# First self attention of a four-layer decoder: scores of each 64-token block only, in both partition halves of a bank

## Time and profile before

| | |
|---|---|
| runs (3), median | 5675.01 us (5669.7 to 5678.21) |
| profiled execution | 5677.53 us |
| its span | 5675.8 us |
| mean granted TensorE clock | 0.904 |
| busy over the span | PE 81%, PEld 48%, DVE 71%, ACT 51%, POOL 47% |
| the changed stage | about 6 to 243 us of the span |

### The profile page before, as it was taken

The page is one execution under the profiler, slowest core; times in us unless marked ns, Lnnn a source line. Parts: engine busy times, 40 slices in busy tenths (PEclk is TensorE's granted clock), DMA queues, the critical chain, the costliest instruction groups (busy, mean ns, idle before and its releaser), DMA issues. The chain is left out here.

```text
span 5675.8 us, 84931 instructions
## 1 busy us (share of the span) xinstructions
PE 4620.5 (81%) x29487; PEld 2737.2 (48%) x29488; DVE 4017.7 (71%) x7585; ACT 2867.0 (51%) x4722; POOL 2669.3 (47%) x2453
## 2 busy tenths in 40 slices
PE   8769999999999999777845776766797679976577
PEld 6555666666666666424632222222464344424344
DVE  4348888888888888576366999999663336548445
ACT  3326777777777777463333545454463325533211
POOL 7437676766776677342074666666432201001100
PEclk9789999999999999887867999999998769977788
DMA  1000000000000000000000000000000000011000
GB/s 21 15 24 1 1 1 25 1 21 1 21 1 21 1 1 5 1 1 2 12 0 14 0 0 0 0 0 0 15 1 1 9 8 19 1 48 25 5 16 7
DMA packets 76485, 49.99 MB, mean 9 GB/s; under 512 B 27879, under 2 KB 71159, under 8 KB 75319
## 3 DMA queue, kind: packets, MB, share of 16 engines
q1 hardware_dynamic: 74039, 43.77, 3.0%
q0 software_dynamic: 2048, 1.05, 0.1%
HBM read 40.18 MB, written 1.18 MB: 7 GB/s over the span
## 5 line engine op out<-in xcount | busy, mean ns | idle before, releaser
L4051 POOL TENSOR_TENSOR l_attn_read<-l_attn_state,l_attn_c_rows 128x1024 f32<-128x1024 f32 x256 | 604.5, 2361 | 329.7 <-DVE l_attn_state L3954 328.7
L2945 POOL TENSOR_TENSOR l_ffn_t<-l_ffn_t 128x512 f32<-128x512 f32 x384 | 489.1, 1274 | 515.2 <-DVE l_ffn_t L2812 515.2
L3954 DVE TENSOR_TENSOR_SCAN l_attn_state<-l_attn_decay,psum 128x1024 f32<-128x1024 f32 x256 | 584.9, 2285 | 8.1
L2546 PE MATMUL psum<-l_ffn_wq,l_ffn_xsT 128*128 128x512 f32 x1152 | 566.2, 600 | 12.4 <-DVE l_ffn_t L2812 10.9
L3756 PE MATMUL psum<-l_attn_read,ident 128*128 128x512 f32 x1024 | 493.0, 604 | 5.4 <-DVE l_attn_yz L3962 3.0
L3747 PE MATMUL psum<-l_attn_parts,pick 96*128 96x512 bf16 x512 | 200.6, 394 | 312.8 <-DVE psum L3946 312.8
L2956 POOL TENSOR_TENSOR l_ffn_p<-l_ffn_p,l_ffn_sm 128x512 f32<-128x512 f32 x384 | 399.6, 1041 | 61.0 <-DVE l_ffn_sm L2844 45.1
L2951 POOL TENSOR_TENSOR l_ffn_t<-l_ffn_t,l_ffn_ss 128x512 f32<-128x512 f32 x384 | 401.0, 1044 | 0.7 <-DVE l_ffn_ss L2827 0.7
L3873 ACT COPY l_attn_c_rows<-psum 128x512 f32<-128x512 f32 x256 | 149.9, 586 | 468.2 <-PE psum L3747 466.7
L2808 DVE TENSOR_TENSOR l_ffn_t<-psum,l_ffn_tab 128x512 f32<-128x512 f32 x384 | 263.6, 686 | 106.5 <-ACT l_ffn_sq L2693 104.7
L3946 DVE TENSOR_TENSOR psum<-psum,l_attn_du 128x1024 f32<-128x1024 f32 x256 | 315.6, 1233 | 32.7 <-POOL l_attn_du L4028 4.6
(11 more groups left out here) (895 smaller groups left out, 11551.8 us busy)
## 6 DMA issues: line engine op xcount, KB each, us to landing
l_ffn_wq<-in_L_ffn_Wqkv SPq DMA_DIRECT2D x6, 1536.0 KB, 6.2
l_xattn_toep<-s4d_taps SPq DMA_DIRECT2D x4, 2048.0 KB, 17.7
l_ffn_wo<-in_L_ffn_Wo SPq DMA_DIRECT2D x6, 512.0 KB, 7.6
l_ffn_w<-in_L_ffn_W SPq DMA_DIRECT2D x6, 341.0 KB
l_ffn_w<-in_L_ffn_w SPq DMA_DIRECT2D x3, 512.0 KB, 4.2
x_all<-in_x SPq DMA_DIRECT2D x4, 256.0 KB, 4.4
l_attn_k<-l_attn_dense_k POOLq DMA_DIRECT2D x64, 16.0 KB, 1.9
l_attn_q<-l_attn_dense_q SPq DMA_DIRECT2D x64, 16.0 KB
```

The costliest lines, as they stand in the source:

```text
L2546: nc.tensor.matmul(ring[it % 2], xsT[:, n % 2, m % G, :], wq[:, z, i * 512:(i + 1) * 512], start=True, stop=True).then_inc(itemed, 1)
L2945: nc.gpsimd.tensor_tensor(t1[:, m % G, i, :], t1[:, m % G, i, :], t2[:, x % 3, :], ALU.add).then_inc(added, 1)
L3954: nc.vector.tensor_tensor_scan(state[:, k % 3, :], decay[:, k % 3, :, :, :].rearrange("p h g t -> p (h g t)"), drive, 0.0, ALU.mult, ALU.a ...
L4051: nc.gpsimd.tensor_tensor(read[:, k % 3, :].rearrange("p (h n) -> p h n", h=2), state[:, k % 3, :].rearrange("p (h n) -> p h n", h=2), row ...
```

## The change

For the local case, each 128 x 128 matrix of scores is replaced by its two diagonal 64 x 64 blocks. Block z (tokens 64z to 64z+63) is written to partitions 64z to 64z+63 of the bank, in columns i*64 to i*64+63 for batch i. A bank then has 256 used columns instead of 512, and each matmul of 128 by 128 becomes two of 64 by 64, for both parts. The mask is 128 x 64 (the same triangle in both halves) and the mask matmuls have 256 columns. VectorE's maximum reads 256 columns. ScalarE's exponential becomes two activations, one for each half of the partitions, which write the diagonal blocks of `pT`. GpSimd sets the whole of `pT` to zero once, behind the masks, and ScalarE waits for that before its first exponential; nobody writes the other blocks afterwards. `value` is as before.

```
-            half_mask, half_mask_t = sb("mask", [128, T]), sb("mask_t", [128, T])
-            mask16, mask_t16 = sb("mask16", [128, T], BF16), sb("mask_t16", [128, T], BF16)
+            half_mask, half_mask_t = sb("mask", [128, CS]), sb("mask_t", [128, CS])
+            mask16, mask_t16 = sb("mask16", [128, CS], BF16), sb("mask_t16", [128, CS], BF16)
...
-                            nc.tensor.matmul(K.bank[n % 2], K.ident16[:], rows(mask16[:], G), start=True, stop=False, skip_group_check=True)
+                            nc.tensor.matmul(K.bank[n % 2][:, 0:G * CS], K.ident16[:], rows(mask16[:], G), start=True, stop=False, skip_group_check=True)
...
-                    for i in range(G):
+                    pieces = [(i, z, slice(CS * z, CS * z + CS)) for i in range(G) for z in range(2)] if local else [(i, 0, slice(0, T)) for i in range(G)]
+                    for i, z, half in pieces:
+                        width = CS if local else NK
...
-                            last = nc.tensor.matmul(K.bank[index(*a) % 2][:, i * NK:i * NK + NK], q4[r, g % 2, s, i * T:i * T + T],
-                                                    k4[r, g % 2, s, i * NK:i * NK + NK], start=not local, stop=True, skip_group_check=local)
+                            keys = k4[r, g % 2, s, i * NK:i * NK + NK]
+                            last = nc.tensor.matmul(K.bank[index(*a) % 2][half, i * width:i * width + width], q4[r, g % 2, s, i * T:i * T + T][:, half],
+                                                    keys[:, half] if local else keys, start=not local, stop=True, skip_group_check=local)
...
-                            last = nc.tensor.matmul(K.bank[2 + index(*b) % 2][:NK, i * T:i * T + T], k4[r, g % 2, s, i * NK:i * NK + NK],
-                                                    q9[r, s, i * T:i * T + T], start=not local, stop=True, skip_group_check=local)
+                            last = nc.tensor.matmul(K.bank[2 + index(*b) % 2][rows_, i * wide:i * wide + wide], keys[:, half] if local else keys,
+                                                    q9[r, s, i * T:i * T + T][:, half], start=not local, stop=True, skip_group_check=local)
...
-                    nc.scalar.activation(pT[:NK, n % 8, :], K.bank[2 + n % 2][:NK, :], ACT.Exp, scale=scale).then_inc(exped, 1)
+                    if local:
+                        if n == 0:
+                            act.wait_ge(masks, 2)
+                        for z in range(2):
+                            half = slice(CS * z, CS * z + CS)
+                            ins = nc.scalar.activation(pT[half, n % 8, :].rearrange("p (b q) -> p b q", b=G)[:, :, half],
+                                                       K.bank[2 + n % 2][half, 0:G * CS].rearrange("p (b q) -> p b q", b=G), ACT.Exp, scale=scale)
+                    else:
+                        ins = nc.scalar.activation(pT[:NK, n % 8, :], K.bank[2 + n % 2][:NK, :], ACT.Exp, scale=scale)
+                    ins.then_inc(exped, 1)
...
-                    ps = K.bank[n % 2][:, :KEYS].rearrange("p (b k) -> p b k", b=G)
+                    ps = K.bank[n % 2][:, :G * (CS if local else NK)].rearrange("p (b k) -> p b k", b=G)
...
-                        build(nc.gpsimd.affine_select(out=full[:], in_=full[:], compare_op=ALU.is_ge, fill=NEG, base=0,
-                                                      pattern=[[sign, T]], channel_multiplier=-sign))
-                        if turned:
-                            build(nc.gpsimd.memset(full[0:CS, CS:T], NEG))
-                        else:
-                            build(nc.gpsimd.memset(full[CS:T, 0:CS], NEG))
+                        for z in range(2):
+                            part = full[CS * z:CS * z + CS, :]
+                            build(nc.gpsimd.affine_select(out=part, in_=part, compare_op=ALU.is_ge, fill=NEG, base=0,
+                                                          pattern=[[sign, CS]], channel_multiplier=-sign))
...
                     nc.gpsimd.memset(to_next[0:CS, CS:T], 0.25 / CS).then_inc(masks, 1)
+                    nc.gpsimd.memset(pT[:], 0.0).then_inc(masks, 1)
```

More of the change, by code:

```diff
@@ L883, in scores @@
                         if local:
-                            nc.tensor.matmul(K.bank[2 + n % 2], K.ident16[:], rows(mask_t16[:], G), start=True, stop=False, skip_group_check=True)
-                    for i in range(G):
+                            nc.tensor.matmul(K.bank[2 + n % 2][:, 0:G * CS], K.ident16[:], rows(mask_t16[:], G), start=True, stop=False, skip_group_check=True)
+                    pieces = [(i, z, slice(CS * z, CS * z + CS)) for i in range(G) for z in range(2)] if local else [(i, 0, slice(0, T)) for i in range(G)]
+                    for i, z, half in pieces:
+                        width = CS if local else NK
                         if a is not None:
@@ L888, in scores @@
                             r = slice(ROW * j, ROW * j + ROW)
-                            last = nc.tensor.matmul(K.bank[index(*a) % 2][:, i * NK:i * NK + NK], q4[r, g % 2, s, i * T:i * T + T],
-                                                    k4[r, g % 2, s, i * NK:i * NK + NK], start=not local, stop=True, skip_group_check=local)
-                            if i == G - 1:
+                            keys = k4[r, g % 2, s, i * NK:i * NK + NK]
+                            last = nc.tensor.matmul(K.bank[index(*a) % 2][half, i * width:i * width + width], q4[r, g % 2, s, i * T:i * T + T][:, half],
+                                                    keys[:, half] if local else keys, start=not local, stop=True, skip_group_check=local)
+                            if (i, z) == pieces[-1][:2]:
                                 last.then_inc(a_done, 1)
@@ L895, in scores @@
                             r = slice(ROW * j, ROW * j + ROW)
-                            last = nc.tensor.matmul(K.bank[2 + index(*b) % 2][:NK, i * T:i * T + T], k4[r, g % 2, s, i * NK:i * NK + NK],
-                                                    q9[r, s, i * T:i * T + T], start=not local, stop=True, skip_group_check=local)
-                            if i == G - 1:
+                            keys = k4[r, g % 2, s, i * NK:i * NK + NK]
+                            rows_ = half if local else slice(0, NK)
+                            wide = CS if local else T
+                            last = nc.tensor.matmul(K.bank[2 + index(*b) % 2][rows_, i * wide:i * wide + wide], keys[:, half] if local else keys,
+                                                    q9[r, s, i * T:i * T + T][:, half], start=not local, stop=True, skip_group_check=local)
+                            if (i, z) == pieces[-1][:2]:
                                 last.then_inc(b_done, 1)
```

## The result

The changed kernel takes 5649.93 us (median of 8 runs, 5643.89 to 5660.41), the one before on the same chip 5670.12. The ratio is 0.9963, 95% interval 0.9952 to 0.9973: 21 us faster, 15 to 27. Of the 9.3 us between 5659.2 and 5649.93, 4.9 come from the kernel before, whose median is 5670.12 over eight runs where the forecast started from 5675.0 over three; so on which side of 5650 the time falls is chance.

What follows compares the result with a forecast made beforehand. TensorE was taken to set the first self attention's pace, but for three standstills. Group gains 14.8 plus tail 3.5, minus 1.0 for memset and 1.5 for clock, gave 15.8 us: 5659.2 us as a median, range 5650 to 5675.

Steps and rivals of the forecast that it cites:

- masks' 0.21 us a slot: TensorE's two mask matmuls, 512 to 256 columns: 0.21 us saved per slot at full clock.
- what slots 6 to 39 win is lost: Group 0 on TensorE: no gain from these slots, since GpSimd's chain to 112.03 us doesn't shorten.
- The longer exponential is covered: ScalarE: two activations take about 0.8 us, 0.2 more than one, hidden because a group still lasts some 40 us.
- The shortened slots no longer cover q: VectorE's evacuation of q, 3.3 us, outlasts two shortened slots of 3.1 us: 1.0 us charged a group.
- the score beat: TensorE's score matmuls as four tiles side by side, 0.056 us a beat for 0.112: 0.35 us a slot, bounds 0 to 0.45.
- the rival that starts bind: TensorE bound by starting matmuls, not columns: only masks won, 3 to 7 us, 5668 to 5672; chance 0.25.
- the memset: GpSimd's new memset of `pT` overlaps VectorE's of `v`, delaying GpSimd's chain by 0 to 2.4 us; 1.0 charged.
- the fixed latency from `fin` to `apply`: TensorE's waits after `fin` of groups 1 and 2: fixed delay of moments, rstd and apply, so shortened slots there gain nothing.
- resumes at 117.9 as before: TensorE after group 0's `fin`: reaches its standstill some 20 us earlier, yet restarts no sooner, plus 1.0 us.
- the long standstill: TensorE's group 0 wait: after 20 us of idling the clock is low at once, 1.5 us lost (0 to 4).
- the 6.3 in place of 3.5: Tail slots 72 to 75, `b` alone, mostly at the lower clock: forecast gain 4 x 0.87 = 3.5 us.
- the 1.2 GHz from 20 to 51 us: TensorE's clock before the change, cited for a rival: clock stays low, some 18 us slower, 5693; chance 0.10.

Runs made afterwards that it cites:

- the first pair: First profiles of the unchanged and changed kernels: last rstd at 240.11 and 213.56 us, executions 5677.53 and 5650.99 us.
- the second pair: Both kernels profiled once more, without further edits: last rstd at 237.5 us before and 212.1 after the change, spans 5669.1 and 5644.0 us.
- the later comparison: The changed kernel timed once more, without further edits, against the kernel before: ratio 0.9951 (0.9938 to 0.9965).
- run 64: Not a label of a follow-up run: "run" is the verb here, four tiles run 64 columns of 32-bit data in 0.06 us each.

## Why the prediction was right or wrong

**Right.** TensorE bounds the stage, and a slot gets shorter by masks and scores. The masks' 0.21 us a slot is measured twice: 2.11 to 1.90 in the old kernel, 1.43 to 1.65 in the new. GpSimd's chain holds group 0 at 112 us, so what slots 6 to 39 win is lost but for the 2.35 us below, in 20.3 us of standstill; taking the taps away brings the rstd 17.4 us forward and the resumption 15.1. The longer exponential is covered, but for 0.3 us at each of the two short standstills. The shortened slots no longer cover q.

**Too small: the score beat.** I took 0.35 us a slot between 0 and 0.45. With the masks' 0.21, the slot's 2.11 to 1.43 leaves 0.47. The upper end was the right one, and the rival that starts bind fell: 32 records start within about 0.5 us, 15 ns each. The Trainium skill's rule in "TensorE: Matmul & The Clock Gate", section "Wait — 56ns, not 53.3ns?", of at least some 25 ns between starts, does not hold here across tiles. What it says in "TensorEngine Tiling (Array Packing)", Key Properties, that different tiles can work in parallel, does: four records within 0.02 us. Over 26 slots this is 3 us, and about 1 us in the tail.

**Too large: the memset.** I charged 1.0 us for two memsets at once. GpSimd's chain starts at 24.10 against 24.09, so they cost nothing.

**The step that failed.** "Slots 53 to 55 and 69 to 71 lie within the fixed latency from `fin` to `apply`: lost, the standstill grows by 3 x 0.56 = 1.7 us", and for group 0 "resumes at 117.9 as before". The latency wasn't fixed. `apply` stands in ScalarE's queue behind an exponential, which waits for TensorE's scores; so the shortened slots count there too, the standstill grew from 2.1 to 2.4 only, and the three resumptions came 2.35, 1.7 and 1.5 us sooner: 5.6 us where I had 0. In group 1, three slots of 0.68 us give 2.04: 1.71 at the resumption, and 0.33 in a longer standstill. That the order of the queue is the cause is shown by moving `apply` alone, in both kernels (the table of rstd to resumption). The row was to be had before: `apply` started at 116.34, 2.4 us after the rstd it was supposed to wait for, and directly behind an exponential.

**The clock.** 1.5 us was charged to the long standstill. In fact the stretch at 1.2 GHz behind it ended at 123 instead of 126, and since TensorE resumed earlier the loss was small. In the tail of the first pair the last `fin` (L977, L981) took 2.0 us instead of 3.7; that and the beat make the 6.3 in place of 3.5, and in the second pair, where it took 2.0 in both kernels, the tail gained 4.2. How the clock falls is partly chance (the standstill of 2.12 us at 167 us, with the lower clock behind it in the first profile and without it in the kernel before with the taps later), so this part of the sum can't be had to a microsecond. One reading of the prediction needs a word: for the 1.2 GHz from 20 to 51 us it has the lengths of rows, while the clock column of that profile reads 1.00 there. The lengths are right (L936 takes 2.08 us at 46.91 and 1.12 at 87.84), and in the profile of the kernel before with the taps later, which has the same distances there, the column reads 0.50.

Together: 5.6 for the resumptions, 1.0 for the memset, the rest, some 4 us, beat and clock: 26.55 instead of 15.8 in the profiles. How the 4 us are shared between beat and clock is an estimate. The times say 21 (15 to 27) and, in the later comparison, 28 (20 to 35).

## What to carry to other kernels

Before a wait is called a fixed latency, look at what stands ahead of the releasing instruction in its own engine's queue: if that waits for the engine which you speed up, the wait shrinks with it. A short standstill of TensorE is to be priced with the stretch at the lower clock behind it; `apply` ahead of one exponential on ScalarE was worth 14 us (8 to 20) here in the old kernel. And a faster engine shows the next chain: the gain of the first group was there to be had only after GpSimd's side work had been moved.

## What the runs showed of the hardware

- Four tiles of 32x64 start within 0.02 us and run 64 columns of 32-bit data in 0.06 us each, for eight beats on end: 15 ns for each pair of weight load and matmul record.
- TensorE's clock behind `fin`'s standstills, over all thirteen profiles: behind 13 of 2.38 to 2.57 us it fell each time, behind 12 of 2.08 to 2.12 us 11 times, behind the one of 1.59 us too, behind 5 of 1.01 and 1.02 us never. The stretches at 1.2 GHz were 3.4 to 10 us long behind groups 0 and 1, and 10 to 44 us behind group 2, where the tail's waits follow. The length of a standstill alone doesn't decide: the waits of 0.9 and 0.4 us at slots 32 and 48 were followed by 1.2 GHz in 8 of 10 cases.
- A memset of 128x4096 on GpSimd takes 3.50 us beside one of the same size on VectorE, and VectorE's takes 3.47 us with it as without it. GpSimd's without VectorE's was not run.
- Two executions of one kernel on one core differ by 5 to 7 us in this program of 5.65 ms, some 4 us of it behind the first stage; a change of 6 us that a slot's length shows at once isn't seen in five rounds of times.
